# Eight of 36 softmax-maxima matmuls moved behind the projected rows, and the transposition of the maxima moved into the first transform

## The reference, cut to what matters

```python
x = x + _L0_conv_ref(_gn(x), ...)      # four 7-tap depthwise directions, attention over them, 3x3 conv
x = x + _L1_conv_ref(_gn(x), ...)      # below

q, k, v = jnp.split(conv1x1(x, w_qkv), 3, axis=1)
q = softmax(q, axis=-1)                # over all 9216 pixels: needs each channel's maximum
k = softmax(k, axis=-1)                # the same
context = einsum('bhdn,bhen->bhde', k, v)
...
x_fft = fftn(x).real
x_mid = gelu(conv1x1(x_fft, w_q1))     # "projected rows", then the first transform
qf = ifftn(conv1x1(x_mid, w_q2)).real
```

## Time and profile before

| | us |
|---|---|
| three runs: lowest, median, highest | 4177.42, 4215.52, 4221.92 |
| span of the profiled execution, first to last instruction | 4236.6 |
| PE busy | 3960.8 (93%) |
| DVE busy | 3033.4 (72%) |
| ACT busy | 1695.8 (40%) |
| mean granted PE clock | 0.906 |

### The profile page before, as it was taken

How to read it: one execution, slowest core, us unless ns; L and a number is a source line. 1 busy time by engine, 2 the same in 40 slices (tenths; PEclk the granted TensorE clock), 3 DMA queues, 4 the chain that set the end, 5 groups by cost and what they waited for, 6 DMA issues and landing times.

```text
span 4236.6 us, 56479 instructions
## 1 busy us (share of the span) xinstructions
PE 3960.8 (93%) x21202; PEld 3254.3 (77%) x21202; DVE 3033.4 (72%) x2829; ACT 1695.8 (40%) x2912; POOL 209.5 (5%) x376
## 2 busy tenths in 40 slices
PE   4659999999999999999999999999999999999998
PEld 2356879968698687968799686986879687896867
DVE  7988877788677878689777876778886887843020
ACT  3413762247412574127622464215641276203430
POOL 1000000100001000000001000010000000010000
PEclk8879799988799799999999877997999979998779
DMA  4372214712155221822147221552218221350002
GB/s 117 88 177 75 61 41 84 188 51 70 29 133 134 52 69 29 202 73 61 41 97 179 56 61 27 126 143 50 71 26 201 74 63 41 76 137 12 1 3 31
DMA packets 164716, 344.11 MB, mean 81 GB/s; under 512 B 110336, under 2 KB 110576, under 8 KB 164432
## 3 DMA queue, kind: packets, MB, share of 16 engines
q1 hardware_dynamic: 141392, 255.36, 24.5%
q0 software_dynamic: 23040, 84.95, 9.1%
HBM read 189.27 MB, written 150.99 MB: 80 GB/s over the span
## 4 chain that ended last, share of the span: by engine, by line
PE 84%; DVE 9%; ACT 3%; issue 3%; DMA 1%; POOL 0%; SPq 0%; DVEq 0%; ACTq 0%; POOLq 0%
PE banks L936 14%; PE banks L937 14%; PE banks L942 14%; PE banks L961 12%; PE banks L951 6%; PE banks L1003 6%; PE banks L967 5%; DVE feat L702 4%; PE banks L968 4%; PE banks L974 3%; PE banks L1013 3%; DVE e_lo L725 2%; PE banks L990 1%; ACT z L529 1%; DMA feat<-feats_d 1%
## 5 line engine op out<-in xcount | busy, mean ns | idle before, releaser
L702 DVE SCALAR_TENSOR_TENSOR feat<-xin,w,feat 96x1536 f32<-96x1536 f32 x540 | 943.6, 1807 | 28.0 <-ACT feat L488 26.9
L936 PE MATMUL banks<-e_hi,a_hi 96*96 96x384 f32 x1728 | 597.7, 346 | 40.9 <-ACT a_hi L572 40.9
L936 PE MATMUL banks<-e_hi,wp_hi 96*96 96x384 f32 x1728 | 587.7, 341 | 24.2 <-DVE x L780 12.1
L961 PEld LDWEIGHTS banks<-mats,z 96*96 96x96 f32 x3072 | 537.8, 259 | 90.2 <-issue 71.0
L937 PE MATMUL banks<-e_lo,a_hi 96*96 96x384 f32 x1728 | 595.2, 345 | 0.0
L937 PE MATMUL banks<-e_lo,wp_hi 96*96 96x384 f32 x1728 | 586.7, 340 | 0.0
L702 DVE SCALAR_TENSOR_TENSOR feat<-xin,wv,feat 96x1536 f32<-96x1536 f32 x288 | 520.7, 1808 | 79.4 <-ACT feat L488 79.4
L702 DVE SCALAR_TENSOR_TENSOR feat<-xin,wh,feat 96x1536 f32<-96x1536 f32 x288 | 520.6, 1808 | 70.1 <-ACT feat L488 69.2
L961 PE MATMUL banks<-mats,z 96*96 96x96 f32 x3072 | 531.5, 347 | 9.8 <-ACT z L529 9.8
L500 ACT ACTIVATE sqjunk<-feat 96x1536 bf16<-96x1536 f32 x192 | 284.1, 1480 | 228.8 <-DVE feat L702 225.5
L563 ACT ACTIVATE res<-banks 96x768 f32<-96x768 f32 x96 | 77.6, 808 | 727.9 <-PE banks L942 727.9
(11 more groups left out here) (145 smaller groups left out, 5261.1 us busy)
## 6 DMA issues: line engine op xcount, KB each, us to landing
feats_d<-feat SPq DMA_DIRECT2D x160, 576.0 KB, 4.1
feat<-feats_d SPq DMA_DIRECT2D x160, 576.0 KB, 6.5
feat<-in_x SPq DMA_DIRECT2D x48, 576.0 KB, 6.9
res<-in_x POOLq DMA_DIRECT2D x96, 288.0 KB, 4.0
out<-x POOLq DMA_DIRECT2D x96, 288.0 KB, 2.8
out<-res POOLq DMA_DIRECT2D x96, 288.0 KB, 4.4
xin<-in_x SPq DMA_DIRECT2D x32, 792.0 KB, 9.1
xin<-in_x SPq DMA_DIRECT2D x16, 684.0 KB, 10.1
```

The lines of the kernel that those rows point to most:

```text
L702: dve.scalar_tensor_tensor(out=dst, in0=src, scalar=taps_w[d](k), in1=dst, op0=ALU.mult, op1=ALU.add).then_inc(tap_done, 1)
L936: pe.matmul(dst, whi[:, t, :], rows(e_hi, a0, n, dx), start=(t == CENTRE_FIRST[0]), stop=False)
L961: last = pe.matmul(ps[0:H, c * W:(c + 1) * W], z[:, :, 4 * g + c], w_dft, start=(c == 0), stop=(c == 3), skip_group_check=True)
```

## The change

Of the 36 uses for the maxima, 28 keep their place. The last eight (`LATE_MAX`) come behind the 24 uses of the rows and directly ahead of the first transform. `max_use` translates the number of a maximum into its use, and `evacs_to` counts the uses that ACT has read. The transposition of `nmax` stands at use 8 of the first transform (`ROW_AT`) on PE, and `max_row` at the same place on ACT. The places of `unit_work` are counted so that each stays at the same use of the rows or the transform as before. DVE's program keeps its order: the waits of its last eight maxima now name later uses. PE also waits for the whole normalised image before the rows.

```diff
+LATE_MAX = 8
-AT_ROWS = U_MAX
-AT_DFT1 = AT_ROWS + U_ROWS
+AT_ROWS = U_MAX - LATE_MAX
+AT_DFT1 = U_MAX + U_ROWS
...
+def max_use(n):
+    return n if n < AT_ROWS else n + U_ROWS
+
+def evacs_to(u):
+    return u - AT_ROWS + 1 if u < AT_ROWS + U_ROWS else u - U_MAX + 1
...
+ROW_AT = 8
@@ ACT @@
             def stage(i, u):
-                n, after = divmod(u - UNIT_AT, UNIT_USES)
+                n, after = divmod((u if u < AT_DFT1 else u - LATE_MAX) - UNIT_AT, UNIT_USES)
@@ ACT @@
             def dft(i, at, ch0, func):
                 for n, (kind, g) in enumerate(DFT_ORDER):
+                    if at == AT_DFT1 and n == ROW_AT:
+                        max_row(i)
...
                     u_rows(i)
-                    max_row(i)
                     dft(i, AT_DFT1, 0, ACT.Gelu)
@@ DVE @@
             def maxes(i, n0, n1):
                 for n in range(n0, n1):
-                    dve.wait_ge(stage_full, i * USES + n + 1)
+                    dve.wait_ge(stage_full, i * USES + max_use(n) + 1)
@@ PE @@
             def dft(i, at):
                 for n, (kind, g) in enumerate(DFT_ORDER):
+                    if at == AT_DFT1 and n == ROW_AT:
+                        pe.wait_ge(l1_small, i * L1_SMALL + 1)
+                        pe.matmul(small_ps[0:1, 0:C], nmax[:, 0:1], ident, start=True, stop=True).then_inc(l1_ps, 1)
@@ PE @@
             def attention_block(i, between):
-                maxes(i)
+                maxes(i, 0, AT_ROWS)
+                pe.wait_ge(xn_ready, (i + 1) * XN)
                 for g in range(U_ROWS):
...
-                pe.wait_ge(l1_small, i * L1_SMALL + 1)
-                pe.matmul(small_ps[0:1, 0:C], nmax[:, 0:1], ident, start=True, stop=True).then_inc(l1_ps, 1)
+                maxes(i, AT_ROWS, U_MAX)
                 dft(i, AT_DFT1)
```

More of the change, by code:

```diff
@@ L81 @@
 UNIT_USES, UNIT_AT = 20, AT_ROWS + 8
-assert UNIT_AT + (LEAD - 2) * UNIT_USES <= AT_E
+assert UNIT_AT + (LEAD - 2) * UNIT_USES <= AT_E - LATE_MAX
+ROW_AT = 8
 SUMS_AFTER = (0, 0, 0, 1, 1, 1)
@@ L709, in maxes @@
                 for n in range(n0, n1):
-                    dve.wait_ge(stage_full, i * USES + n + 1)
-                    dve.tensor_reduce(mx[:, n % 2, n // 2:n // 2 + 1], stage_ps[0:C, n % SLOTS, :], AX.X, ALU.max)\
+                    dve.wait_ge(stage_full, i * USES + max_use(n) + 1)
+                    dve.tensor_reduce(mx[:, n % 2, n // 2:n // 2 + 1], stage_ps[0:C, max_use(n) % SLOTS, :], AX.X, ALU.max)\
                         .then_inc(max_part, 1)
@@ L905, in stage @@
                     pass
-                elif v < U_MAX:
+                elif v < AT_ROWS:
                     pe.wait_ge(max_part, i * U_MAX + v + 1)
+                elif AT_ROWS + U_ROWS <= v < AT_DFT1:
+                    pe.wait_ge(max_part, i * U_MAX + v - U_ROWS + 1)
                 else:
-                    pe.wait_ge(stage_evac, i * (USES - U_MAX) + v - U_MAX + 1)
+                    pe.wait_ge(stage_evac, i * (USES - U_MAX) + evacs_to(v))
                 return stage_ps[:, u % SLOTS]
             def evacuated(i, u):
-                pe.wait_ge(stage_evac, i * (USES - U_MAX) + u - U_MAX + 1)
+                pe.wait_ge(stage_evac, i * (USES - U_MAX) + evacs_to(u))
             def group_sums(b, chain, done):
@@ L943, in conv, with maxes @@
                     last.then_inc(done, 1)
-            def maxes(i):
-                for n in range(U_MAX):
+            def maxes(i, n0, n1):
+                for n in range(n0, n1):
                     t = n // 2
                     pe.wait_ge(xn_ready, i * XN + t + 1)
-                    ps = stage(i, n)
+                    ps = stage(i, max_use(n))
                     w = wkv[0:C, 0:C] if n % 2 == 0 else wq
@@ L958, in dft @@
                         if g == 0:
-                            evacuated(i, at - 1)
+                            evacuated(i, AT_ROWS + U_ROWS - 1 if at == AT_DFT1 else at - 1)
                         for c in range(4):
```

## The result

The changed kernel takes 4321.12 us (median of 4 runs, 4313.49 to 4354.17), the kernel before 4218.72 us (median of 4, 4177.42 to 4255.25): a ratio of 1.029, interval 1.019 to 1.039. Two further comparisons gave 1.033 (1.029 to 1.037) and 1.030 (1.023 to 1.037). The forecast was 4278 us with a range from 4240 to 4316 us: the direction was right, the size too small.

What follows compares the result with a forecast made beforehand. PE was taken to bound the kernel, busy 93% of the span. Seven images at 8.0 us of delay plus 1.0 us of clock, less 0.4 us, made 62.6 us on 4215.5: 4278 us, range 4240 to 4316 us.

Steps and rivals of the forecast that it cites:

- Points 1 and 2: PE ahead of the first transform: late maxima close the gap, gaining 1.6 us; the transposition's 0.33 us at use 8 is covered.
- Point 3: DVE at its last eight maxima: idles nearly 15 us per image, and the taps of unit 2 start 16.4 us later.
- Point 4: First transform: ACT's square waits 14.3 us for DVE's tap; PE idles 9.2 us before use 9, 8.0 us later net.
- Point 5: Later in the image: no second ACT wait, by 3 us; DVE's 21.9 us do not shrink; PE's 8.0 us stay.
- Point 6: PE's granted clock in the first transform: nearly unchanged, 1 us per image slower, with ends of 5.1 and -8.0 us.
- The clock term: First transform: 1 us per image added for PE's granted clock, on top of 8.0 us of delay.
- Nearly the same mixture: First transform behind use 9: clock recovers at nearly as varied times as before, a little slower, 1 us per image.
- the bound of 5.1 us: First transform behind use 9: extra cost per image if the pause keeps the clock down throughout, 47.8 us against 42.7.
- The last image: Image without taps and squares: only the 0.41 us gap ahead of its first transform goes, 0.4 us gained.
- The one in which the clock recovers behind each pause: First transform: its long piece behind the pause runs at full clock, giving 4215 to 4255 us; chance 0.14.
- The one in which the closed gap matters: Ahead of the first transform: no wait at the square, clock stays up, 81 us saved, 4134 us; chance 0.03.
- The one that paid the wait more fully: First transform: PE loses about 13 us per image through banks, clock or unit 3's squares, 4306 us; chance 0.18.

Runs made afterwards that it cites:

- e2: Changed kernel with ACT's work on units 2 to 6 put twelve uses later, DVE left as it was: 4196.68 us, ratio 0.988 to the kernel before.
- e1: Changed kernel with DVE running the first eight taps of unit 2 before its last eight maxima: 4197.54 us, ratio 0.984 to the kernel before.
- e5: Changed kernel with DVE running four taps of unit 2 before its last eight maxima: 4292.99 us, ratio 1.024 to the kernel before.
- e4: Changed kernel with eight taps ahead of the late maxima and the transposition back ahead of the first transform: 4234.38 us, ratio 1.004 to the kernel before.
- x3: Kernel before with one more product, result unused, at use 8 of the first transform: 4308.64 us, ratio 1.022 to the kernel before.

## Why the prediction was right and wrong

*Points 1 and 2, the gain ahead of the transform: right.* 1.6 us forecast, 2.1 us in the means of three profiles. The transposition at use 8 is hidden in the pause, as said; what it does to the clock is another matter (below).

*Point 3, DVE: right.* Nearly 15 us of idle time forecast, 14.77 us measured, and free by itself (e2).

*Point 4, ACT's square and PE's pause: right in mechanism and in the time of use 9.* ACT's wait was forecast at 14.3 us and is 14.50 us. Use 9 was to come 1943.2 - 1919.2 = 24.0 us after the start of the transform, and comes after 24.2 us. The pause is 11.9 instead of 9.2 us, because the clock stayed up in the first uses and PE reached its full banks 2.7 us sooner; this gains nothing, since ACT sets the end. In the three images of 21 in which the clock fell within the first uses, the pause is 9.0 us and use 9 comes at the same 24.2 us. e1, e2 and e5 show the chain: with 0, 4 and 8 taps ahead the pause is 11.9, 5.0 and 0 us, and in e2 it is gone though DVE is as late.

*Point 5: right.* In the fourth image DVE still waits 21.9 us ahead of the attention weights, as before, and the second wait of ACT, forecast to be missed by 3 us, does not occur: there is no idle time ahead of its square.

```profile
DVE ctxm L729 <- PE banks L1017: 21.9, 1, 21.9
```

```profile
2019.63 1.47 ACT L496 ACTIVATE sqjunk<-feat 96x1536 bf16<-96x1536 f32 x1
```

*Point 6, the clock in the first transform: about right in size, with some luck.* Up to keys and values the forecast had 8.0 + 1.0 = 9.0 us per image; the means of three profiles give 11.7 - 2.1 = 9.6 us. The clock term within it was 1 us; behind use 9 the changed kernel needs 70.4 - 24.2 = 46.2 us on average where the forecast had 42.7 + 1.0 us. "Nearly the same mixture" was too kind: 17 of the 21 images needed 47.2 to 47.6 us, 4.5 to 4.9 us above 42.7, near the bound of 5.1 us. The sum came out because the kernel before needs more than 42.7 us there too, 44.4 us in the mean of its three profiles, so that only some 2 us per image are due to this term. The Trainium skill ("TensorE: Matmul & The Clock Gate", section "Part 1: The HAM clock gate") has an idle TensorE fall to half rate and busy work lift it again. The first half held here: the clock fell within the pause (0.67 over it, 0.50 behind it). The second did not in the image shown: PE was busy for 46.91 of the 47 us behind the pause and stayed at 0.50.

*The step that failed* is the scope of point 6. It let the clock act on the first transform alone ("This decides the length of the first transform") and took the rest of the image as shifted but unchanged. The second transform has the same kinds of product and the same two lengths: 62.8 or 63.2 us against 47.4 us, 16 us per image and mostly 3 us more in the products behind it. In the trace of before it was there to be seen in two of seven images. It went from 2 of 21 images to 13 of 21, +10.1 us per image or +71 us, for which the sum had zero. The last image was the other omission: 0.4 us forecast, 29.8 us gained, since without a gap or a pause its first transform ran at full clock (46.8 us against 62.1 to 62.2) and its second in 50.1 instead of 60.6 to 63.3 us. Together the two account for the miss: 62.6 + 71 - 29 + 4 (0.6 us in each first transform) + 2 (keys and values and the rest) is 110 us, the difference of the mean spans. The stretch up to keys and values, forecast at 7 x 9.0 = 63 us, makes 67 of the 110 us; the rest is mainly the clock in second transforms, whose work the change did not touch.

*The rivals.* The one in which the clock recovers behind each pause did not come; of the 21 images it recovered early in one (37.4 us behind use 9, first image of the first profile) and late in three others (42.7 to 44.0 us against 47.2 to 47.6). The one in which the closed gap matters named a real effect, which the pause then cancelled: in the last image and in five images of e1 the first transform does run at 46.8 us. The one that paid the wait more fully was nearest in time (4306 us); the clock's part of it nearly came, but the second transform stands in none of the rivals.

*What stays open.* Where on the grid the second transform starts sorts 139 of 140 cases into two unbroken groups, but why the clock falls from there and not from elsewhere isn't shown. Nor was a kernel run in which nothing but that place is moved from image to image. The change thus moved the starts to a worse place; that a pause must do so isn't shown, since kernels without any pause had 2, 3, 4 and more of 7 second transforms at half clock, and e4 none.

## What to carry to other kernels

Slack is read at each consumer, not at the end of the engine's work: DVE had 21.9 us to its last reader and 3.7 us to the nearest. Before moving work behind a wait, list what is queued behind the waiting instruction and who waits for the first of it; giving DVE eight taps to do ahead of that wait turned 2.9% slower into slightly faster. And where the profile shows a stage at either of two lengths by TensorE's clock, price every such stage of the image, also those behind the change; with such a stage, a difference of 2% between two kernels may be nothing but that, so compare the lengths of each stage at equal clock before blaming an edit. Look also at when the stage starts relative to the changes of the clock: an experiment that alters the length of an image moves this too.

## What was not expected of the hardware

- The granted clock stayed at 0.50 for 61 us of unbroken PE work in a transform (x3, 951 to 1012 us), where the records of the 96x96 products follow each other every 0.16 us, each with its weight load. In profiles of kernels that differ by a single product of 0.3 to 0.4 us (x3 and before) the first transform took over 62 us in seven of seven images against three to five, and the second in seven against none to two. The whole effect is 2.2% in the time.
- The clock changes only at the points of an evenly spaced grid, and the place on it at which a second transform starts sorted full from half clock in 139 of 140 cases of the seven images with both parts.
- Twelve 96x512 products (10.3 us at full clock) followed by 1.6 us of idle time left the transform as slow as 11.9 us of idle time did in four images of six (71.0 and 71.4 us); fourteen without a gap left it at full clock in seven of seven images.
- Runs of the same unedited kernel differ with the granted clock: 4161.71 us at a mean of 0.942 in one group and 4245.12 us at 0.904 in another.
